# Bias rows by one-row matmuls on TensorE instead of adds on GpSimd and VectorE, in a four-layer transformer kernel

## The reference

```python
# layer 0, first block: gated convolution and a state-space scan
y = y * sigmoid(g) + silu(v)
y = y @ out_w + out_b                     # outb
# layer 1: linear attention
qkv = xn @ qkv_w + qkv_b                  # vb is the last third
# layer 3, first block: token mixing and a decaying scan
out = einsum('bsd,ed->bse', states, W_out) + b_out      # bout3
# layer 3, second block: multi-head attention, 16 heads
qkv = x @ wi.T + bi                       # bv3 is the last third
x = layernorm(x + (o @ wo.T + bo))        # bo3
```

## Time and profile before

| | |
|---|---|
| median of 3 runs | 3761.51 us (3755.66 to 3767.43) |
| profiled execution | 3767.43 us, span 3765.6 us |
| busy in the span | PE 2676.4 (71%), PEld 1969.2 (52%), DVE 2456.0 (65%), ACT 1771.2 (47%), POOL 647.4 (17%) |
| DMA, mean | 70 GB/s |
| granted TensorE clock, mean | 0.871 |
| GpSimd adds of a `spread` row (L744, L2474, L1868) | 3 x 16, median 1.27 to 1.48 us each |

### The profile page before, as it was taken

One profiled execution on the slowest core, in us unless ns is written; L12 is line 12 of the kernel. 1 busy time (PEld: TensorE's weight loads), 2 busy tenths in 40 slices (PEclk: granted clock), 3 DMA queues, 4 the chain that ended last, 5 costly groups with the idle time before them and its releaser, 6 DMA issues. The chain is left out here.

```text
span 3765.6 us, 82319 instructions
## 1 busy us (share of the span) xinstructions
PE 2676.4 (71%) x21527; PEld 1969.2 (52%) x21527; DVE 2456.0 (65%) x6571; ACT 1771.2 (47%) x4634; POOL 647.4 (17%) x943
## 2 busy tenths in 40 slices
PE   0354786999977687997329999986554999984170
PEld 0133463348977555997216777776331555544160
DVE  5662788227878533776757777755886888866267
ACT  5330541333454354665225666752242777762243
POOL 0000110000000187665000000000220000001773
PEclk9987987999998598998779999978796999995595
DMA  9139300110000111222685554500085555530123
GB/s 212 24 82 265 95 27 0 34 33 0 0 1 2 63 47 48 64 67 80 182 218 67 68 67 63 68 9 1 0 260 106 70 66 64 68 47 22 49 77 100
DMA packets 348794, 264.81 MB, mean 70 GB/s; under 512 B 20504, under 2 KB 331208, under 8 KB 348040
## 3 DMA queue, kind: packets, MB, share of 16 engines
q1 hardware_dynamic: 326944, 227.12, 30.3%
q0 software_dynamic: 12928, 26.70, 2.1%
q10 hardware_dynamic: 8704, 8.39, 0.7%
HBM read 145.70 MB, written 114.86 MB: 69 GB/s over the span
## 5 line engine op out<-in xcount | busy, mean ns | idle before, releaser
L2129 PE MATMUL h_ps<-h_sk,h_sq 128*128 128x256 bf16 (+1 forms) x2048 | 408.4, 268 | 116.2 <-DMA h_vb<-v_ones 100.2
L2144 PE MATMUL h_ps<-h_sq,h_sk 128*128 128x256 bf16 (+1 forms) x2048 | 394.3, 262 | 35.9 <-issue 14.8
L2061 DVE TENSOR_REDUCE h_mx<-h_ps 128x2 f32<-128x512 f32 x512 | 333.9, 684 | 83.7 <-PE h_ps L2129 65.4
L2233 ACT ACTIVATE h_pt<-h_ps 128x512 f32<-128x512 f32 x512 | 286.9, 593 | 66.2 <-PE h_ps L2144 55.2
L2129 PEld LDWEIGHTS h_ps<-h_sk,h_sq 128*128 128x128 bf16 x2048 | 174.8, 99 | 255.0 <-issue 124.7
L1472 POOL TENSOR_TENSOR idle<-idle 128x1 f32<-128x1 f32 x400 | 100.4, 251 | 955.2 <-ACT e_row L1536 883.9
L2230 ACT ACTIVATE h_pt<-h_ps 128x256 f32<-128x256 f32 x512 | 196.3, 383 | 113.4 <-PE h_ps L2147 111.3
L2111 POOL TENSOR_TENSOR h_mpart<-h_mrest,h_mpart 16x256 bf16<-16x256 f32 x64 | 42.3, 661 | 1202.8 <-ACT h_mpart L2259 1202.8
L2159 PE MATMUL h_ps_o<-h_pt,h_vb 128*9 128x256 f32 (+1 forms) x4096 | 243.8, 356 | 0.9 <-ACT h_pt L2233 0.5
L2144 PEld LDWEIGHTS h_ps<-h_sq,h_sk 128*128 128x128 bf16 x2048 | 198.6, 99 | 81.0 <-issue 18.9
L1671 POOL DMA_INDIRECT results<-e_y,e_ykey x208 | 220.8, 1061 | 74.0 <-issue 71.1
(11 more groups left out here) (408 smaller groups left out, 6581.7 us busy)
## 6 DMA issues: line engine op xcount, KB each, us to landing
h_sq<-q_stack SPq DMA_DIRECT2D x64, 384.0 KB
h_sk<-k_stack SPq DMA_DIRECT2D x64, 384.0 KB
sorted_rows<-pad SPq DMA_DIRECT2D x26, 520.0 KB, 11.6
e_xt<-sorted_rows SPq DMA_DIRECT2D x52, 260.0 KB, 2.9
e_got<-results SPq DMA_DIRECT2D x48, 256.0 KB, 4.6
q_stack<-p_parts SPq DMA_DIRECT2D x32, 384.0 KB, 3.1
k_stack<-p_parts SPq DMA_DIRECT2D x32, 384.0 KB, 3.7
v_ones<-p_v SPq DMA_DIRECT2D x32, 288.0 KB, 2.7
```

The lines of the kernel that those rows point to most:

```text
L2061: dve.tensor_reduce(mx[:, h, :], sv, AX, ALU.max).then_inc(s["mx"].sem, 1)
L2129: ins = pe.matmul(o, sq[u][:, h, q * P:(q + 1) * P], sk[u][:, h, 0:nk], start=True, stop=not causal)
L2144: ins = pe.matmul(o[:, q0:], sk[u][:, h, t * P:(t + 1) * P], sq[u][:, h, q0:], start=True, stop=not causal)
L2233: act.activation(to, sv, ACT.Exp, scale=scale).then_inc(s["ex"].sem, 1)
```

## The change

The four bias rows are no longer spread over the partitions. Each of the additions becomes one more matmul of one row (a stationary row of 128 ones, a moving row of 128 biases), the first of its accumulation group: 4 a unit in the layer-0 output stage, in loop s and in p3's v, and 2 a batch in h3, 256 in all. In loop l the 64 matmuls of 128 rows become matmuls of one row. GpSimd's adds go in the layer-0 stage and in loop s; in p3 its add becomes a copy, and VectorE's L1858 a copy from PSUM. The waits for c_biased and s_biased go; L733 waits for c_grown instead. The four matmuls and the copy in the table stage go.

```diff
-            ps_b = bank("ps_b", st)
...
-                    dve.wait_ge(peed, n_pe[0] + 1)
-                    link(dve, dve.tensor_copy(spread[:, :, :].rearrange("p b d -> p (b d)"), ps_b[:, 0, :]))
-
-                @block.tensor
-                def _(pe):
-                    for name, n in SPREAD.items():
-                        ins = pe.matmul(ps_b[:, 0, n * D:(n + 1) * D], c("ones"), c(name), start=True, stop=True)
-                    pe_done(ins)
...
                     def added(n, j, r):
-                        dve.wait_ge(*c_biased.now(n, 1))
+                        dve.wait_ge(*c_grown.now(n, 1))
                         dve.wait_ge(*c_out.now(n, 1))
...
-                @block.gpsimd
-                def _(gp):
-                    def biased(n, j, r):
-                        gp.wait_ge(*c_grown.now(n, 1))
-                        xs = x_res[:, ds(n * UT, UT), :]
-                        gp.tensor_tensor(xs, xs, every_row("outb").unsqueeze(1).to_broadcast([P, UT, D]), ALU.add
-                                         ).then_inc(c_biased.sem, 1)
...
                             dst = ps_o[:, j, t * P:(t + 1) * P]
+                            pe.matmul(dst, c("ones", rows=1), c("outb", rows=1), start=True, stop=False)
                             for b in range(CB):
                                 ins = pe.matmul(dst, sv[j][:, b, t * P:(t + 1) * P], c("outw", b * D, D),
-                                                start=(b == 0), stop=(b == CB - 1))
+                                                start=False, stop=(b == CB - 1))
...
-                            pe.matmul(dst, c("ones"), c("vb"), start=True, stop=False)
+                            pe.matmul(dst, c("ones", rows=1), c("vb", rows=1), start=True, stop=False)
...
-                                bv = w["bv"].rearrange("p (h e) -> p h e", h=NH).unsqueeze(1).to_broadcast([P, UT, NH, HD])
-                                ins = dve.tensor_tensor(to, got, bv, ALU.add)
-                            ins.then_inc(s["vc"].sem, 1)
+                            dve.tensor_copy(v1[j][:, :, :, 0:HD], ps_v[:, 0, :].rearrange("p (t h e) -> p t h e", t=UT, h=NH)
+                                            ).then_inc(s["vc"].sem, 1)
...
-                                gp.tensor_tensor(keep[0][:, ds(n * UT, UT), :], nrm[j][:, :, :],
-                                                 keep[1].unsqueeze(1).to_broadcast([P, UT, D]), ALU.add
-                                                 ).then_inc(s["kept"].sem, 1)
+                                gp.tensor_copy(keep[:, ds(n * UT, UT), :], nrm[j][:, :, :]).then_inc(s["kept"].sem, 1)
...
                             for t in range(UT):
                                 dst = ps_v[:, 0, t * D:(t + 1) * D]
-                                ins = pe.matmul(dst, hT[j][:, t * P:(t + 1) * P], w["v"], start=True, stop=True)
+                                if w["bv"] is not None:
+                                    pe.matmul(dst, c("ones", rows=1), w["bv"], start=True, stop=False)
+                                ins = pe.matmul(dst, hT[j][:, t * P:(t + 1) * P], w["v"], start=(w["bv"] is None), stop=True)
...
                             for t in range(TPB):
                                 o = ps_m[:, 0, t * D:(t + 1) * D]
-                                ins = pe.matmul(o, oT[:, t * P:(t + 1) * P], w["o"], start=True, stop=True)
+                                if w["bo"] is not None:
+                                    pe.matmul(o, c("ones", rows=1), w["bo"], start=True, stop=False)
+                                ins = pe.matmul(o, oT[:, t * P:(t + 1) * P], w["o"], start=(w["bo"] is None), stop=True)
...
                     def added(n, j, r):
                         xs = x_res[:, ds(n * UT, UT), :]
-                        dve.wait_ge(*s_biased.now(n, 1))
                         dve.wait_ge(*s_o.now(n, 1))
...
-                @block.gpsimd
-                def _(gp):
-                    def biased(n, j, r):
-                        gp.wait_ge(*fr_s.nrm.now(n, 1))
-                        xs = x_res[:, ds(n * UT, UT), :]
-                        gp.tensor_tensor(xs, xs, every_row("bout3").unsqueeze(1).to_broadcast([P, UT, D]), ALU.add
-                                         ).then_inc(s_biased.sem, 1)
...
                             o = ps_o[:, j, t * D:(t + 1) * D]
+                            pe.matmul(o, c("ones", rows=1), c("bout3", rows=1), start=True, stop=False)
                             ins = pe.matmul(o, state[j][:, t // TPB, (t % TPB) * P:(t % TPB + 1) * P], c("wout3"),
-                                            start=True, stop=True)
+                                            start=False, stop=True)
```

More of the change, by code:

```diff
@@ L216, in build @@
         idle = sb("idle", [P, 2])
[L217 to L222, removed]
         def link(dve, ins):
@@ L257, in build @@
         c_grown = sig("c_grown", 1)
-        c_biased = sig("c_biased", 1)
-        s_biased = sig("s_biased", 1)
         routes = {}
@@ L737, in _ @@
                     staggered(dve, NU, S, (0, normed), (3, added), (1, gated))
-                @block.gpsimd
-                def _(gp):
-                    def biased(n, j, r):
-                        gp.wait_ge(*c_grown.now(n, 1))
-                        xs = x_res[:, ds(n * UT, UT), :]
-                        gp.tensor_tensor(xs, xs, every_row("outb").unsqueeze(1).to_broadcast([P, UT, D]), ALU.add
-                                         ).then_inc(c_biased.sem, 1)
-                    staggered(gp, NU, S, (0, biased))
                 @block.tensor
@@ L2296, in build @@
             project("p2", x_res, dict(qk=(w_qkv[:, 0, :], w_qkv[:, 1, :]), b=(None, None), v=w_qkv[:, 2, :], bv=None))
-        attend("h2", True, x_res, dict(o=c("wo2")))
+        attend("h2", True, x_res, dict(o=c("wo2"), bo=None))
         stats(x_res)
@@ L2523, in build @@
             project("p3", x_res, dict(qk=(c("wq3"), c("wk3")), b=(c("bq3"), c("bk3")), v=c("wv3"),
-                                      bv=every_row("bv3")), keep=(x2, every_row("bo3")))
-            attend("h3", False, x2, dict(o=c("wo3")))
+                                      bv=c("bv3", rows=1)), keep=x2)
+            attend("h3", False, x2, dict(o=c("wo3"), bo=c("bo3", rows=1)))
             stats(x2)
```

## The result

| | kernel before | changed kernel |
|---|---|---|
| median of 4 runs | 3758.59 us (3752.08 to 3767.43) | 3906.81 us (3901.23 to 3912.76) |
| ratio | | 1.0393, 95% interval 1.0365 to 1.0421 |
| profiled execution | 3767.43 us, span 3765.6 | 3900.78 us, span 3898.9 |
| granted TensorE clock, mean | 0.871 | 0.855 |

The changed kernel is 148 us slower; +55 was predicted, with 3860 as the upper end. The direction is right, the size is not.

The account below looks back on a forecast made before the run. The prediction took VectorE to bound the layer-0 output stage, TensorE h3 and the stores p3. Its terms 7 + 3 + 3 + 9 + 33 gave +55 us, 3816 us against the median 3761.51, range 3785 to 3860.

Parts of the forecast that it names:

- loop s: Layer 3's mixer: added matmuls mostly fit TensorE's idle time; last unit's bare matmuls and a few late units, +3 us.
- p3: Projection p3: TensorE's unit exceeds the stores' 5.8 us, so compute ends later; +9 us, bounds 0 and +39.
- h3: Attention h3: two one-row matmuls a batch, +1.03 us each batch with nothing hiding it; +33 us over 32 batches.
- loop l: Layer 1's attention: matmuls going from 128 rows to one make each batch 0.12 us late; +3 us over 32 batches.
- the clock of loop s and p3: Loop s: TensorE nearly always busy, so the higher clock level expected; p3: unit of 6.43 us, no clock change stated.
- The second rival: Loop s half at the lower clock, +10 to +30; loop l hiding nothing, +22; both 3850 to 3870 us; chance 0.12.
- A unit at the higher level: TensorE's unit in p3: claimed 6.43 us with the added matmuls, against 5.55 before.
- The price of 0.61 us: All stages: TensorE time of one added one-row matmul, taken from L1566; lower bound 0.22 us, upper 0.61.
- The fourth rival: Row count doesn't matter, price 0.22 us everywhere: -12 layer-0 output, 0 l, s, p3, +14 h3; 3764 us; chance 0.06.
- Layer-0 output: Layer-0 output stage: VectorE's contention goes, but TensorE takes over as bound at 8.09 us a unit; +7 us.
- the first rival: h3: later groups absorb what the projection's group loses, so half of 33 us goes; 3800 us; chance 0.10.
- The third rival, faster: Layer-0 output gains 12 us at price 0.22, and h3 hides its 0.45 a batch; 3750 us; chance 0.02.

Follow-up runs that it names:

- e5: Changed kernel with 64 rows instead of one in all five bias matmuls; 3908.68 us, beside 3824.73 for the kernel before.
- e8: Changed kernel plus four unread 128-row matmuls of 512 columns per unit in p3; ratio 1.0422 to the kernel before.
- e7: Changed kernel with each unit's one-row matmuls merged into one wide one (also per batch in h3), loop l left; ratio 1.0067 to the kernel before.
- e1: Changed kernel with 128 rows in all five bias matmuls; ratio 1.0015 to the kernel before, +6 us.
- e11: Kernel before with 128-row bias matmuls replacing GpSimd's adds in the layer-0 output stage and loop s; ratio 0.9983.
- e13: Changed kernel with 65 rows in all five bias matmuls; 3765.87 us, beside 3751.74 for the kernel before.
- e15: Kernel before with 128-row bias matmuls replacing GpSimd's adds in the layer-0 output stage alone; ratio 0.9984.
- e12: Changed kernel with 96 rows (layer-0 output, p3), 113 (loops s, l) and 97 (h3); 3834.75 us, beside 3830.30 for the kernel before.

## Why the prediction was wrong, and where it was right

**The step that failed is the clock of loop s and p3.** For loop s the prediction said "TensorE will be busy nearly all the time, so I expect the higher level", and for p3 it added the one-row price to a unit at the higher level without a word on the clock. TensorE was busy nearly all the time, and was granted 0.60 and 0.57: +33.9 us in loop s instead of 3 and +67.7 in p3 and its stores instead of 9, 90 of the 93 us that the sum was short. Busy time was the wrong thing to look at. With the same stalls, 1, 32 and 64 rows give 0.57, 0.70 and 0.86 in p3; with the same one-row matmuls, more full-row work gives 0.78 to 0.94. Once the level is low, a unit gets longer and holds less full-row work per time, which goes the same way; how far this feeds the fall isn't shown. The second rival came near in loop s: half its units at the lower level, "+10 to +30", against +33.9 measured with 6 of 15 distances there. But it took that level for what was left over from before, not for what the added matmuls bring, and it had nothing for p3, where twice as much went; with its +22 for loop l, which didn't come, it still ends at 3870, 37 us short.

How much of the two stages is clock and how much is price comes from 64 rows, which pay the full price. Loop s takes 95.0 us against 91.6: +3.4 for the price, at a clock of 0.91, and +30.5 for one row's clock. p3's compute takes 127.7 against 94.7: +33 for the price, the missed wait and a few units at the lower level, of which 15 x (7.05 - 5.55) = 22 would come at the higher level throughout; the other +39, up to the 166.5 of one row, are the clock.

**p3 had a second, smaller error.** A unit at the higher level is 7.05 us, not 6.43 (e5, and e8: 10.48 with its four fillers of 0.86). The wait for VectorE's copy of v was in the trace of before, where the same copy, L1858, ends 1.13 us of waiting that lie beside the stores, and I dropped it when I made TensorE the bound. 15 x 0.62 is 9 us.

**The price of 0.61 us was right**, in every stage at the higher level, and the rows of before that it came from were the right ones. The Trainium skill's rule (TensorE: Matmul & The Clock Gate, "Why this matters for your kernels"), by which a single small-K matmul takes the time of one with K=128, agrees with these runs from 65 rows on. Up to 64 rows it holds for a pass by itself (e7: two one-row passes of 512 columns take some 0.43 us each, as with 128 rows), but not for what the matmul costs between 128-row ones: 0.61 us instead of 0.22. The fourth rival is what the kernel with 128 rows did: forecast +2 with -12, 0, 0, 0, +14, measured +6 with -12, -2, -2, +4, +15.

**Layer-0 output, loop l and h3 were right** at +7.5, +1.6 and +34.8 against 7, 3 and 33. Loop l took 157 or 160 us in the kernels with the same one-row code in it, and 153 to 155 in those with 128 rows, so the +3 is within what it does. The first rests on two opposite terms, and e1 shows them singly: without GpSimd's adds and at a price of 0.22 the stage gains 12 us, so the contention of the two engines was as large as the earlier trace rows says; at 0.61 TensorE takes it back and 7 more. In h3 each batch pays, and no later group gives it back: the first rival is refuted at 64 rows and at one.

**The third rival, faster**, needed a price under 0.31 and an h3 that hides its part. With 65 rows or more the first condition holds, the second doesn't: h3 pays 15 us. Leave h3, p3 and loop l alone (e11), and the kernel is faster, by 7 us.

## What to carry to other kernels

A bias, mask or constant added by a matmul of one row costs nearly three times a 128-row one of the same columns when it alternates with 128-row matmuls: pad it with zero rows to at least 65, or write the whole bank's bias with one wide matmul (measured here with f32 and 128 columns). Even a padded one is 0.22 us of TensorE: it gained 12 us where VectorE was the bound beside GpSimd's add, and cost 15 us in h3, where TensorE is. Before TensorE is given more to do in a stage, don't ask only whether it will be busy, but what it will be busy with: in a stage with little full-row work, few-row matmuls can bring the clock down to near its 1.2 GHz level, and every other matmul of the stage pays. And when an engine becomes the bound, its waits that were hidden before have to go back into its unit.

## What the runs showed of the hardware that I had not expected

- The step of the price is between 64 and 65 rows, with f32: 1.05 against 0.67 us for one bias matmul and the four passes behind it, and the same for 1, 32 and 64 rows.
- TensorE's busy time doesn't tell the granted clock; the rows that take part matter. Loop s was granted 0.60 with TensorE busy 117.55 of 122 us (one row), 0.91 with 86.36 of 92 (64 rows), and 0.90 with 62.01 of 87 (128 rows). The same page of the Trainium skill ("Why this matters for your kernels") ties the clock's fall to idle gaps of TensorE; here loop s has no gap over 0.1 us between matmuls after its first units and p3 none over 0.86, and both were low most of the time.
- Adding work can shorten a stage: 32 passes more in p3, and 17 us less.
- Chips differ in one place. The kernel before takes 3752 to 3762 us in the first runs and on the chip of e13 to e15, and 3823 to 3830 on the two chips of e1 to e12. The sorted experts of layer 1 take 491 to 493 us in the profiles of the former and 543 to 565 in all of the latter, whichever kernel ran; of the five stages of the change, those left as they were take the same on all within 3 us.
